# A fused decoder layer on one Trainium2 core: the transposes of x1 and x2 move from TensorE to crossbar DMAs

## The reference

```python
x = _layernorm(x + attn(x, Wq, Wk, Wv, fc_w, fc_b))        # 3 heads of width 512, softmax, mean over heads
x = _layernorm(x + xattn(x, ctx, Wq, Wkv_expand, Wout))    # 16 heads of width 32, causal, keys and values from ctx
x = _layernorm(x + ffn(x, gate_w, w_gate, w_up, w_down, sh_gate, sh_up, sh_down))  # top 6 of 64 experts, and a shared one
```

## Time and profile before

| | |
|---|---|
| median of 3 runs | 2055.86 us |
| lowest and highest | 2055.02 and 2065.52 us |
| span of the profiled execution | 2064.9 us; the run nearest to it is that of 2065.52 us, 0.6 us more, taken as its own time |
| PE (TensorE matmuls) busy | 1989.4 us, 96% |
| PEld (its weight loads) busy | 1227.9 us, 59% |
| DVE (VectorE) busy | 1674.1 us, 81% |
| ACT (ScalarE) busy | 1026.7 us, 50% |
| POOL (GpSimd) busy | 740.1 us, 36% |
| DMA | 268.84 MB, mean 130 GB/s |

### The profile page before, as it was taken

One profiled execution on the slowest core, in us unless ns is written; L12 is line 12 of the kernel. 1 busy time (PEld: TensorE's weight loads), 2 busy tenths in 40 slices (PEclk: granted clock), 3 DMA queues, 4 the chain that ended last, 5 costly groups with the idle time before them and its releaser, 6 DMA issues.

```text
span 2064.9 us, 43350 instructions
## 1 busy us (share of the span) xinstructions
PE 1989.4 (96%) x16976; PEld 1227.9 (59%) x16976; DVE 1674.1 (81%) x3877; ACT 1026.7 (50%) x1569; POOL 740.1 (36%) x710
## 2 busy tenths in 40 slices
PE   8999999999999999999999997899999999999998
PEld 3666666676676666666666664455555555555553
DVE  5557988988988988898898898848887788878867
ACT  5425434444453453553444455435665556566545
POOL 1003223223323323323322322434565555564633
PEclk9999999999999999999999998999999999999999
DMA  6700110011011011011101113479998999999948
GB/s 224 79 24 16 41 55 32 25 55 50 17 45 55 12 45 55 12 45 55 32 24 55 45 52 104 163 204 276 307 283 257 283 292 299 300 286 298 293 92 320
DMA packets 134439, 268.84 MB, mean 130 GB/s; under 512 B 32699, under 2 KB 42939, under 8 KB 134236
## 3 DMA queue, kind: packets, MB, share of 16 engines
q1 hardware_dynamic: 110108, 226.06, 33.2%
q0 software_dynamic: 24128, 40.01, 9.9%
HBM read 208.67 MB, written 57.42 MB: 129 GB/s over the span
## 4 chain that ended last, share of the span: by engine, by line
PE 48%; DVE 31%; DMA 8%; issue 6%; ACT 4%; POOL 2%; POOLq 0%; DVEq 0%; ACTq 0%
PE moe_bank L1710 18%; PE ring L918 17%; DVE quad L1298 6%; DMA expert_sums<-tion_then_expert_weights,scatter_index 6%; DVE inv_denominator L1314 4%; PE moe_bank L1779 3%; DVE scratch L1262 3%; PE fold L485 3%; DVE stats L1223 2%; DVE scratch L1308 2%; PE quad L1033 1%; DVE maxima L1298 1%; DMA expert_sums<-tion_then_expert_weights 1%; ACT scratch L1180 1%; POOL scratch L888 1%
## 5 line engine op out<-in xcount | busy, mean ns | idle before, releaser
L178 POOL DMA_INDIRECT slot_table<-table_records,slot_of_choice x204 | 205.3, 1006 | 493.2 <-PE ring L918 403.4
L1160 ACT ACTIVATE scratch<-ring 128x512 f16<-128x512 f32 x224 | 131.6, 594 | 323.4 <-PE ring L918 323.1
L918 PE MATMUL ring<-xT_split,tion_then_expert_weights 128*128 128x256 f16 x2304 | 267.3, 273 | 0.0
L918 PE MATMUL ring<-tion_then_expert_weights,xT_split 128*128 128x512 f16 x1152 | 264.6, 379 | 0.0
L918 PEld LDWEIGHTS ring<-xT_split,tion_then_expert_weights 128*128 128x128 f16 x2304 | 220.5, 98 | 38.9 <-issue 10.3
L888 POOL TENSOR_SCALAR_AFFINE_SELECT scratch<-scratch 128x1024 f32<-128x1024 f32 x64 | 95.5, 1493 | 312.2 <-ACT scratch L1180 309.2
L1659 POOL DMA_INDIRECT expert_sums<-tion_then_expert_weights,scatter_index x64 | 136.0, 2125 | 181.1 <-PE moe_bank L1710 59.2
L918 PEld LDWEIGHTS ring<-tion_then_expert_weights,xT_split 128*128 128x128 f16 x1152 | 110.2, 98 | 125.8 <-DVE scratch L1262 3.0
L1298 DVE CUSTOM_DVE_ANT_0 quad<-quad,causal_penalty 128x128 f32<-128x128 f32 (+1 forms) x512 | 165.1, 393 | 1.7 <-PE quad L1016 1.7
L1262 DVE SCALAR_TENSOR_TENSOR scratch<-ring,scratch 128x512 f16<-128x512 f32 x192 | 127.8, 684 | 42.3 <-ACT scratch L1160 40.8
L918 PE MATMUL ring<-scratch,xT_split 128*128 128x256 f16 x1152 | 136.0, 272 | 10.7 <-DVE maxima_T L1305 6.4
(11 more groups left out here) (251 smaller groups left out, 4034.0 us busy)
## 6 DMA issues: line engine op xcount, KB each, us to landing
gate_up_landing<-in_w_gate SPq DMA_DIRECT2D x43, 704.0 KB, 5.7
gate_up_landing<-in_w_up SPq DMA_DIRECT2D x43, 704.0 KB, 5.9
scratch<-in_w_down SPq DMA_DIRECT2D x43, 512.0 KB, 4.4
scratch<-in_w_gate SPq DMA_DIRECT2D x21, 704.0 KB, 5.5
scratch<-in_w_up SPq DMA_DIRECT2D x21, 704.0 KB, 5.6
tion_then_expert_weights<-in_w_down SPq DMA_DIRECT2D x21, 512.0 KB, 4.8
scratch<-in_w_down SPq DMA_DIRECT2D x43, 192.0 KB, 5.8
xT_in<-in_xT SPq DMA_DIRECT2D x16, 512.0 KB, 5.0
```

What stands on the lines that cost most here:

```text
L178: pool.indirect_dma_start(self.dram, bass.IndirectOffsetOnAxis(ap=self.slot[:, tb, c:c + 1], axis=0), self.record[:, tb, c, :], None, boun ...
L918: last = pe.matmul(out_, left(a, c), right(b, c), start=(n == 0 and not onto), stop=(n == 3 * chunks - 1))
L1160: act.activation(half(0), src, ACT.Copy, scale=scale).then_inc(high, 1)
```

## The change

Steps T and TX go. In their place ScalarE writes the high half of x1 and x2 in row layout (XH, ZH), VectorE the low half (XL, ZL), and SyncE issues crossbar transposes of fp16 data from SBUF to SBUF, one for each block of 128 rows by 1024 values. LN2 is cut in two, and both parts move behind the body's start: ST2 (means and variances), then, behind V00, the inverse roots. All lists are written anew. The new lists begin:

```diff
 PE_BODY = [
-    ("V", 0, 0), ("Y", 0, 0), ("T", 0, 0), ("T", 1, 0), ("K", 0, 0), ("K", 1, 0), ("C", 0, 0), ("Q", 0, 0),
-    ("Q", 1, 0), ("TX", 0, 0), ("V", 0, 1), ("M", 0, 0), ("Y", 0, 1), ("TX", 1, 0), ("M", 1, 0), ("S", 0, 0),
+    ("V", 0, 0), ("Y", 0, 0), ("K", 0, 0), ("K", 1, 0), ("C", 0, 0), ("V", 0, 1), ("Q", 0, 0),
+    ("Q", 1, 0), ("Y", 0, 1), ("M", 0, 0), ("S", 0, 0), ("M", 1, 0),
     ("S", 0, 1), ("R", 0, 0), ("M", 2, 0), ("Y", 1, 0), ("C", 1, 0), ("V", 1, 0), ("M", 3, 0), ("Y", 1, 1),
 ACT_BODY = [
-    ("V", 0, 0), ("NX1", 0, 0), ("Y", 0, 0), ("T", 0, 0), ("T", 1, 0), ("K", 0, 0), ("C", 0, 0), ("K", 1, 0),
-    ("Q", 0, 0), ("NX2", 0, 0), ("Q", 1, 0), ("TX", 0, 0), ("V", 0, 1), ("Y", 0, 1), ("TX", 1, 0), ("S", 0, 0),
+    ("NX1", 0, 0), ("XH", 0, 0), ("XH", 1, 0), ("V", 0, 0), ("Y", 0, 0), ("K", 0, 0), ("K", 1, 0), ("C", 0, 0),
+    ("V", 0, 1), ("NX2", 0, 0), ("ZH", 0, 0), ("Q", 0, 0), ("Q", 1, 0), ("Y", 0, 1), ("S", 0, 0),
 DVE_BODY = [
-    ("V", 0, 0), ("Y", 0, 0), ("T", 0, 0), ("T", 1, 0), ("C", 0, 0), ("K", 0, 0), ("Q", 0, 0), ("K", 1, 0),
-    ("TX", 0, 0), ("Q", 1, 0), ("V", 0, 1), ("M", 0, 0), ("Y", 0, 1), ("TX", 1, 0), ("M", 1, 0), ("S", 0, 0),
-    ("S", 0, 1), ("R", 0, 0), ("S1", 0, 0), ("M", 2, 0), ("Y", 1, 0), ("C", 1, 0), ("RC", 0, 0), ("M", 3, 0),
+    ("ST2", 0, 0), ("XL", 0, 0), ("XL", 1, 0), ("V", 0, 0), ("LN", 2, 0), ("Y", 0, 0), ("K", 0, 0), ("K", 1, 0),
+    ("C", 0, 0), ("V", 0, 1), ("Q", 0, 0), ("ZL", 0, 0), ("Q", 1, 0), ("Y", 0, 1), ("M", 0, 0), ("S", 0, 0),
+    ("M", 1, 0), ("S", 0, 1), ("R", 0, 0), ("S1", 0, 0), ("M", 2, 0), ("Y", 1, 0), ("C", 1, 0), ("RC", 0, 0), ("M", 3, 0),
...
-    ("LN", 2, 0),
 ]
```

From ("Y", 1, 0) on, the lists of a body are as before. In the tail (body 17) ZH follows NX2, and R waits for the transposes of ZH's and ZL's output. The code of the new steps:

```diff
+            if b.b:
+                for t in range(NB):
+                    sp.wait_ge(x1_split, b.n(0, NB, 0, t + 1))
+                    sp.dma_start_transpose(x1s[:, :, :, t * P:(t + 1) * P].rearrange("p a c n -> p (a c) n"),
+                                           x1r[:, t, :, :].rearrange("p a e -> p (a e)")).then_inc(x1T_in, 16)
...
             if b.c:
-                sp.wait_ge(ln2, b.n(0, 0, 1, 1))
+                sp.wait_ge(ln2, b.n(0, 0, NB, NB))
                 for d in (x2_d, moe_d):
                     sp.dma_start(d[...], x2[:, :, :]).then_inc(x2_stored, 16)
-                sp.wait_ge(free, b.freed("TX", 1, 0))
+                sp.wait_ge(x2T_stored, b.n(0, 0, 16, 1))
+                sp.wait_ge(x2_split, b.n(0, 0, 1, 1))
+                for t in range(NB):
+                    sp.dma_start_transpose(x2s[:, t, :, :, :].rearrange("p a c n -> p (a c) n"),
+                                           x2r[:, t, :, :].rearrange("p a e -> p (a e)")).then_inc(x2T_in, 16)
+                sp.wait_ge(x2T_in, b.n(0, 0, 32, 32))
                 sp.dma_start(x2T_d[...], x2s[...]).then_inc(x2T_stored, 16)
...
                 elif name == "Q":
-                    pe.wait_ge(free, b.freed("T", 1, 0))
+                    pe.wait_ge(x1T_in, b.n(0, 32, 0, 32))
...
                 elif name == "R":
-                    pe.wait_ge(free, b.freed("TX", 1, 0))
+                    pe.wait_ge(x2T_in, b.n(0, 0, 32, 32))
...
+                elif name == "XH":
+                    act.wait_ge(ln1, b.n(0, NB, 0, g + 1))
+                    if not b.is_(1):
+                        act.wait_ge(x1T_in, b.n(0, 32, 0, 0))
+                    act.activation(x1r[:, g, 0, :], src[:, g, :], ACT.Copy).then_inc(x1_high, 1)
...
+                elif name == "ZH":
+                    act.activation(x2r[:, :, 0, :], x2[:, :, :], ACT.Copy).then_inc(x2_high, 1)
...
+                elif name == "XL":
+                    dve.wait_ge(x1_high, b.n(0, NB, 0, g + 1))
+                    dve.tensor_tensor(x1r[:, g, 1, :], src[:, g, :], x1r[:, g, 0, :], ALU.subtract)\
+                       .then_inc(x1_split, 1)
+                elif name == "ZL":
+                    dve.tensor_tensor(x2r[:, :, 1, :], x2[:, :, :], x2r[:, :, 0, :], ALU.subtract)\
+                       .then_inc(x2_split, 1)
```

More of the change, by code:

```diff
@@ L595 @@
 A_STEPS = {"Y", "V", "S", "S1", "S2", "O", "XS"}
-C_STEPS = {"NX2", "TX", "R", "RC", "RM", "CT", "RS", "SC"}
+C_STEPS = {"NX2", "ZH", "ZL", "ST2", "R", "RC", "RM", "CT", "RS", "SC"}
 SHARED_STEPS = {"WS", "SG", "GC", "SU", "SH"}
@@ L767, in high @@
         def high(self, *step):
-            return done_before(self.i, 12, 8, 2) + (self.split.index(step) + 1)
+            return done_before(self.i, 12, 6) + (self.split.index(step) + 1)
         def n(self, per_a, per_b, per_c, extra):
@@ L773, in bank @@
         def bank(self, *step):
-            return bank[self.ring.index(step) % RING]
+            return bank[(jobs_before(self.i) + self.ring.index(step)) % RING]
         def reuse(self, eng, *step):
@@ L1093, in halves @@
             return o[:, :], lambda a: v[:, a, g, h, :], 1.0
-        if name == "T":
-            return two, lambda a: x1s[:, a, 2 * g:2 * g + 2, :], 1.0
         if name == "Q":
@@ L1151, in emit @@
                     for t in range(NB):
-                        last = act.activation(x2[:, t, :], pre2[:, t, :], ACT.Identity,
-                                              scale=rstd[:, NB + t:NB + t + 1], bias=shift[:, NB + t:NB + t + 1])
-                    last.then_inc(ln2, 1)
+                        act.activation(x2[:, t, :], pre2[:, t, :], ACT.Identity,
+                                       scale=rstd[:, NB + t:NB + t + 1], bias=shift[:, NB + t:NB + t + 1])\
+                           .then_inc(ln2, 1)
+                elif name == "ZH":
+                    act.wait_ge(ln2, b.n(0, 0, NB, NB))
+                    if not b.is_(2):
+                        act.wait_ge(x2T_in, b.n(0, 0, 32, 0))
+                    act.activation(x2r[:, :, 0, :], x2[:, :, :], ACT.Copy).then_inc(x2_high, 1)
                 elif s in b.split:
                     act.wait_ge(full, b.job(*s))
-                    if name == "TX" and g == 0:
-                        act.wait_ge(x2T_stored, b.n(0, 0, 16, 1))
                     src, half, scale = halves(name, g, h, b.bank(*s))
@@ L1216, in link, with row_stats, row_scales @@
                 dve.wait_ge(dve_step, done_before(b.i, LINKS_A, LINKS_B, LINKS_C) + (1 + links[0]))
-            def row_scales(n0, src2, scaled):
-                n1 = n0 + NB
-                rows = [(n0 + t, src2[:, t, :]) for t in range(NB)]
-                for n, src in rows:
-                    last = dve.bn_stats(stats[:, n, :], src)
+            def row_stats(n0, src2):
+                for t in range(NB):
+                    last = dve.bn_stats(stats[:, n0 + t, :], src2[:, t, :])
                 link(last)
                 own_wait(dve, taken)
-                for n, _ in rows:
-                    last = dve.bn_aggr(mv[:, n, :], stats[:, n, :])
+                for t in range(NB):
+                    last = dve.bn_aggr(mv[:, n0 + t, :], stats[:, n0 + t, :])
                 link(last)
+            def row_scales(n0, scaled):
+                n1 = n0 + NB
                 inverse_root(dve, link, rstd[:, n0:n1], mv[:, n0:n1, 1], root_tmp[:, :, n0:n1])
@@ L1255, in emit @@
                     src, half, scale = halves(name, g, h, o)
-                    if name == "TX":
-                        for t in range(NB):
-                            last = dve.scalar_tensor_tensor(half(1)[:, t], src[:, t], scale,
-                                                            half(0)[:, t], ALU.mult, ALU.subtract)
-                        last.then_inc(free, 1)
-                    else:
-                        dve.scalar_tensor_tensor(half(1), src, scale, half(0), ALU.mult, ALU.subtract)\
-                           .then_inc(free, 1)
+                    dve.scalar_tensor_tensor(half(1), src, scale, half(0), ALU.mult, ALU.subtract)\
+                       .then_inc(free, 1)
                 elif name == "S":
@@ L1389, in on_vector @@
         bodies(dve, emit)
+    tail_freed = [None] * RING
+    for b in (Body(B), Body(B + 1)):
+        for n, s in enumerate(b.ring):
+            tail_freed[(jobs_before(b.i) + n) % RING] = (s_copied, s[1] + 1) if s[0] == "SG" else (free, b.freed(*s))
     return Stage(on_sync, on_gpsimd, on_scalar, on_vector, on_tensor, dict(
-        tail_freed=[(free, Body(B + 1).freed(*s)) for s in Body(B + 1).ring],
+        tail_freed=tail_freed,
         quad_freed=[(s_silu, EARLY), (s_prod, EARLY), (s_prod, 3), (s_prod, 4)],
@@ L1897, in on_vector @@
         dve.wait_ge(*layers["early_split"])
+        dve.wait_ge(table.ready, B + 1)
         for step in MOE:
```

63 lines of the change are left out of this document (31 added, 32 removed), and 17 rows, old and new, of tables (ACT_LAST, DVE_LAST, PE_LAST).

## The result

The changed kernel takes 2092.24 us (median of 4 runs, 2084.68 to 2113.27), the kernel before beside it 2060.69 us (4 runs, 2055.02 to 2093.04): the ratio is 1.0155, with a 95% interval of 1.0098 to 1.0212. It is slower, by more than forecast (0.9%).

The account below looks back on a forecast made before the run. The prediction took the chain of waits through VectorE, not TensorE's busy share, as the bound. Fourteen bodies at +0.89 us (+12.5), body 1 +2.6, body 16 0 and the tail +3.7 gave +18.8 us: 2075 us, range 2044 to 2112.

Parts of the forecast that it names:

- the forecast's own span: The likeliest case alone, whole kernel slower at 2066 to 2092 us; chance 0.46.
- The handover: Start of each body: VectorE lets TensorE start V01 2.12 us later than K0 started before.
- TensorE's stretch: In each body V01, Q0, Q1, Y01 take 10.45 us against 10.41 before: plus 0.04.
- VectorE's run to Y11: Later in each body VectorE loses V01's split (0.61 us) and TX1 (0.66): minus 1.27.
- Body 1: First body, without LN2: later V01, one split saved, x1's pair landing 1.1 us behind V01: +2.6 us.
- The crossbar: A transpose pair lands 5.0 us after its second issue, hidden at Q0 with 1.4 us to spare.
- The rival of the late crossbar: At Q0: a pair needs 8.4 us, x1 lands 2.0 us behind V01, 39 us more, 2114; chance 0.14.
- The tail: Body 17: x2's pair lands at 1314.1, R was loaded at 1310.43, all passing to the gathered rows: +3.7 us.
- Body 16: x1's pair lands about when Q0 began before, and M0 still waits for VectorE's weight splits: 0.
- TensorE is the bound, faster: If VectorE keeps ahead at V01, M0 and M1, 2.0 us leave every body: 32 us less, 2024; chance 0.20.
- Nothing measurable: VectorE's second run shortens more and the handover costs 1 us less: within 10 us of 2056; chance 0.17.

Follow-up runs that it names:

- Run 1: The changed kernel with LN2 moved behind C0 on VectorE: body 74.70 us, ratio 1.0021 to the kernel before.
- run 4: The changed kernel with each crossbar transpose of x1 issued twice, first into an unread buffer: body 77.06 us, ratio 1.0185 to the kernel before.
- run 5: The changed kernel with LN2 behind C0, M0 ahead of Y01, M1 ahead of S00, M0 waiting only for K0 and Q0: ratio 0.9874 to the kernel before.
- run 6: As run 5, with ZL ahead of Q0's split and the tail's x2 split and transposed block by block: ratio 0.9875 to the kernel before.
- run 7: The body of run 5, the tail block by block with its transposes ahead of the two x2 stores: ratio 0.9870 to the kernel before.

## Why the prediction was right, and where it was off

The sign, the mechanism and its place were right: slower, because VectorE's run ahead of Y00's split grew while TensorE had spare time. Of the marks named: V01's wait is 1.30 us (forecast 1.3) with VectorE's split as the releaser, there is idle time at S00 and M1, and no wait for a DMA at Q0 in the alike bodies. 2092 lies inside the range but at the upper edge of the forecast's own span (2066 to 2092). The sum up to the experts was +18.8 and came out +28.5. That the profiled execution took 2084.68 us, almost the 2084.3 forecast for one, is luck: its experts were 10.5 us shorter than those of the profile before, which hides the miss.

- **The handover: 2.12 forecast, 2.29 measured.** The difference is XL's wait for XH, 0.52 us in place of 0.35. LN2's chain took 2.43 us (2.45). Run 1 took it away, and the body fell by 1.47.
- **TensorE's stretch: +0.04 forecast, +0.23 measured** (660.74 to M0's 671.30 is 10.56 us; before, K0's 645.93 to M0's 656.26 is 10.33). I had taken the ends of the old stretch from the chain, 10.41, and the new one from starts only.
- **VectorE's run to Y11: -1.27 forecast, -1.03 measured** (672.03 to Y11's end, 18.65 us, against 19.68). Of the 0.24 us, 0.14 is a gap ahead of M1's maxima (675.74 to 675.88), for which TensorE's M1 had itself waited. The rest is spread over single instructions. No run took that apart.
- Together a body costs +1.49 instead of +0.89, and the 14 bodies (+21.1 in place of +12.5) hold 8.6 of the 9.7 us missing in the sum. The stretch up to body 1 came out 0.74 us shorter, for which nothing was forecast. **The step that was off is this sum of three small differences**: each was 0.2 us off, all the same way, and 14 bodies multiply them.
- **Body 1: +2.6 forecast, +4.16 measured.** The step left out TensorE's clock: after the 2.54 us of idle at C0, the granted clock was 0.51 from 127 to 130 us, its 1.2 GHz level. C0 took 1.26 us to V01's start in place of 0.64, V01 3.47 in place of 2.61: 1.5 us in all. In the kernel before, an idle time of 1.50 us at the same place left the clock at 1.00. The miss of 1.6 is also smaller than the terms were off: the 1.1 us that I had put down for the crossbar didn't come (no wait at Q0), so 2.7 us were missing, and what the other 1.2 are was not followed.
- **The crossbar: 5.0 us for a pair behind the second issue, 3.2 measured** (3.1 to 4.6). The lower bound, 3.4, was nearer: the reason for taking the load's row, that writing SBUF is the harder side, is not borne out. With 3.2 us the spare time at Q0 came out 2.2 us instead of 1.4. The rival of the late crossbar is out; run 4 shows how close it was. The 1309 ns for a 128x128 block of the Trainium skill's page "VectorE: DVE Perf Modes", section "The three transpose paths", can't be added up block by block: eight blocks in one DMA landed after 3.2 us here, where an estimate from that figure gives 10.5. The 261 GB/s of the Trainium skill's page "DMA: Bandwidth & Descriptors", section "Latency and other measured facts", would by an estimate be 1.0 us for one transpose, which is near the 1.3 us that each holds the queue and far from its landing.
- **The tail: +3.7 forecast, +3.78 measured** up to the gathered rows. The number agrees better than its terms. R came 4.39 us later against OUT0 (20.14 against 15.75). Behind its 7.02 us of idle the granted clock was 0.50, and the 12 matmuls behind R took 4.67 us in place of 2.59. That cost only 0.46, since before TensorE had idled 2.01 us there for R's result. From there to the gathered rows both kernels take 45.90 us. The eight gathered transposes then took 1.11 us and not 2.18, because their rows had landed and the old wait of 0.83 us was gone. The path that I had named, with TensorE waiting for the gathered rows, isn't the one at the end any more.
- **Body 16: 0 forecast, +0.20.** There Q0's wait has another name (6.66 us on the DMA; before, TensorE idled 1.07, 2.51 and 1.50 us at T and Q0) and nearly the same end: Q0 begins 13.96 us behind OUT0 against 13.69. Nothing on GpSimd or in the stores showed.
- **The rival "TensorE is the bound, faster" was wrong for this order and right for another.** Its condition was that Y00's split end before C0 does. Run 1 fulfils it, and yet only reaches 74.70. With M0 earlier and its needless wait gone too (run 5), nearly the gain that the rival forecast, 2.0 us a body, is there (1.8 against before).
- **Nothing measurable** asked for a handover 1 us cheaper. It was 0.17 dearer.

## What to carry to other kernels

When work is taken off the engine that looks full, the order of the lists decides whether the kernel is faster or slower: move what can wait (here LN2's chain) behind the step whose result frees the next bank, above all when something new must stand ahead of that step, and ask of every wait whether it waits for more than is read. Judge a removal in an arrangement that suits it: here the crossbar alone cost 1.5%, the two reordered kernels with TensorE's transposes gained nothing, and both together gained 1.3%. A per-body sum needs its small terms from the same kind of end points on both sides, since the loop multiplies their error.

## What the runs showed of the hardware that was not expected

- A crossbar transpose from SBUF to SBUF of 128x1024 fp16 elements (256 KB) held SyncE's DMA queue 1.24 to 1.47 us for x1 and landed in 3.1 to 4.6 us, close to the plain store of the earlier trace rows, which moves 512 KB and took 3.4. In the tail a pair held the queue 3.84 us when it was issued close behind two stores (run 6), and 2.66 us ahead of them (run 7).
- The 64 transposes brought 67,584 packets under 512 B more (100,283 against 32,699), 1,056 each; the 32 more of run 4 brought 33,792 more, again 1,056 each. In the alike bodies of the changed kernel the trace puts no engine's wait down to a DMA; the DMA share there rose from 0.12 to 0.20.
- TensorE's clock fell to its lower level (0.51, that of 1.2 GHz) after 2.54 us of idle in body 1 and cost 1.5 us there, and again (0.50) after 7.02 us in the tail. The kernel before has such a stretch too: in body 16 it idled 2.51 and 1.50 us with little work between them, and the clock was 0.50 from 1245.7 to 1250 us. The waits of 1.0 to 1.7 us in the alike bodies left it at 1.00.
- The same expert code took 690.4 to 726.8 us in eleven profiled executions. Four of them lie within 690.4 to 690.5. In the others VectorE waits longer for the scatters into `expert_sums`: 1.7 us at most in those four, 27.2 in the kernel before (700.9 us), 65.4 in run 5 (719.2), 71.7 in run 1 (726.8). What makes the scatters late stays open.
